# Absolute step sizes by DVE, one region of token slots per expert, three batches scattered early, and the zero fill on SyncE's queue

## The reference, cut to what matters

```
delta = jax.nn.softplus(dt_raw @ dt_w.T + dt_b)       # per batch, 512 channels x 512 steps
dA = jnp.exp(d_t[:, :, None] * A)
h = dA * h + d_t[:, :, None] * B_t[:, None, :] * x_t[:, :, None]
...
# top-1 mixture: each token goes to the expert with the largest gate logit
e = argmax(x @ gate_W + gate_b);  y = gelu(x @ W1[e] + b1[e]) @ W2[e] + b2[e]
```

## Time and profile before

| | us |
|---|---|
| three runs | 2758.61, 2760.15, 2762.63 |
| profiled execution, its own time | 2750.26 |
| its span | 2748.4 |
| PE busy in the span | 2504.7 (91%) |
| DVE busy | 1437.4 (52%) |
| ACT busy | 1101.9 (40%) |
| POOL busy | 709.6 (26%) |

### The profile page before, as it was taken

One profiled execution on the slowest core, in us unless ns is written; L12 is line 12 of the kernel. 1 busy time (PEld: TensorE's weight loads), 2 busy tenths in 40 slices (PEclk: granted clock), 3 DMA queues, 4 the chain that ended last, 5 costly groups with the idle time before them and its releaser, 6 DMA issues. The chain is left out here.

```text
span 2748.4 us, 40088 instructions
## 1 busy us (share of the span) xinstructions
PE 2504.7 (91%) x16440; PEld 1507.8 (55%) x16441; DVE 1437.4 (52%) x2067; ACT 1101.9 (40%) x1901; POOL 709.6 (26%) x388
## 2 busy tenths in 40 slices
PE   7759999999999999999949977999999998799998
PEld 4346533854375535753348854363453544588887
DVE  5557437952976357843811125555455654644442
ACT  3675335822664256533512223544445443011111
POOL 0148026910964056802720020000000000022222
PEclk9979999999999999999979987999999999899999
DMA  5541002100040003100059940010100102045553
GB/s 203 217 189 40 0 1 103 64 1 0 1 151 17 1 1 127 40 1 0 8 209 338 339 122 12 1 24 23 23 25 1 25 8 93 23 161 166 175 175 83
DMA packets 62127, 219.26 MB, mean 80 GB/s; under 512 B 12293, under 2 KB 28122, under 8 KB 45178
## 3 DMA queue, kind: packets, MB, share of 16 engines
q1 hardware_dynamic: 45802, 187.39, 18.9%
q0 software_dynamic: 9568, 18.75, 2.8%
q10 hardware_dynamic: 6576, 10.57, 1.1%
HBM read 172.50 MB, written 39.99 MB: 77 GB/s over the span
## 5 line engine op out<-in xcount | busy, mean ns | idle before, releaser
L653 PE MATMUL psum<-arena 128*128 128x512 f32 (+4 forms) x3776 | 1036.6, 427 | 59.9 <-ACT arena L1552 11.5
L653 PEld LDWEIGHTS psum<-arena 128*128 128x128 f32 x3776 | 617.4, 194 | 417.8 <-issue 312.5
L2539 POOL TENSOR_TENSOR arena<-arena 128x1024 f32<-128x1024 f32 x128 | 299.6, 2369 | 94.7 <-DVE arena L2019 79.9
L2019 DVE TENSOR_TENSOR_SCAN arena<-arena,psum 128x512 f32<-128x512 f32 x256 | 290.8, 1200 | 22.4 <-PE psum L809 14.6
L809 PEld LDWEIGHTS psum<-arena 128*128 128x128 f32 x2048 | 236.6, 193 | 49.3 <-ACT arena L1582 40.3
L809 PE MATMUL psum<-arena 128*128 128x128 f32 x2048 | 249.0, 279 | 2.0 <-issue 1.9
L2579 POOL DMA_INDIRECT arena<-xn,arena x32 | 31.6, 987 | 778.5 <-DVE arena L2481 771.5
L2546 POOL TENSOR_TENSOR arena<-arena 128x1024 f32<-128x1024 f32 x32 | 76.0, 2374 | 525.3 <-ACT arena L1681 525.3
L2127 DVE SCALAR_TENSOR_TENSOR arena<-psum,arena 128x1024 f32<-128x1024 f32 x128 | 155.9, 1244 | 93.9 <-PE psum L968 93.5
L1860 ACT ACTIVATE arena<-psum 128x256 f32<-128x256 f32 x128 | 49.1, 384 | 296.2 <-PE psum L653 296.2
L1681 ACT ACTIVATE arena<-arena 128x1024 f32<-128x1024 f32 x128 | 147.1, 1149 | 44.3 <-DVE arena L2127 43.0
(11 more groups left out here) (294 smaller groups left out, 3056.6 us busy)
## 6 DMA issues: line engine op xcount, KB each, us to landing
arena<-in_W SPq DMA_DIRECT2D x46, 1024.0 KB
arena<-c_rows SPq DMA_DIRECT2D x32, 512.0 KB, 4.1
arena<-in_Wg SPq DMA_DIRECT2D x16, 1024.0 KB, 4.9
arena<-in_Wu SPq DMA_DIRECT2D x16, 1024.0 KB, 7.5
arena<-in_Wd SPq DMA_DIRECT2D x16, 1024.0 KB, 9.9
arena<-in_xT SPq DMA_DIRECT2D x8, 512.0 KB, 6.0
zs_all<-arena SPq DMA_DIRECT2D x4, 1024.0 KB, 3.9
ut_all<-arena SPq DMA_DIRECT2D x4, 1024.0 KB, 8.8
```

What stands on the lines that cost most here:

```text
L653: r = mm(dst, w, x, start=i == 0, stop=i == len(pairs) - 1)
L2019: V.tensor_tensor_scan(hs[n % 3][:, c, :], dA[n % 2][:, c, :], bank[4 + c], 0.0, ALU.mult, ALU.add)\
L2539: nc.gpsimd.tensor_tensor(h, h, c_all[:, n % CBUFS, :].unsqueeze(1).broadcast_to([P, 2, L]), ALU.mult)\
```

## The change

**Step sizes.** ACT's four Abs of a round go; DVE does them as max(-v, v) directly behind L1962. In round 5, DVE instead of ACT copies batch 2's turned product, and DVE instead of POOL multiplies batch 3's delta by u, tile by tile behind each softplus.

**Slots.** `slots_x` becomes 135 tiles (17.7 MB instead of 3.1 MB): expert e has a region of its own of 2048 rows, so a token's row no longer depends on the counts of all tokens, only on those of earlier batches (`run`). Nine DMAs of 15 tiles each, issued by SP behind batch 0's loads of C, fill it with zeros. The store and load of `xn0` go; `xnn` has memory of its own. While batch b (1 to 3) is in its scans and attention, DVE picks experts and rows of batch b-1 (`pick_expert`, `place_tokens`), PE counts, and POOL scatters its four chunks. After the barrier only batch 3's 512 tokens are left: pick, count, place, four scatters.

**Expert loop.** A tile's rows start where the region says (`row_i`, read into a register), so the token tiles are now loaded by SP (`load_tokens`), ahead of the same tile's weights; ACT's queue has no part in it.

The diff, cut to its core:

```diff
+XT0, ZT0 = E0 * CH + E0 - 1, 9
-        slots_x = dram("slots_x", ((NT0 + 1) * P, D))
+        slots_x, slots_y = dram("slots_x", (XT0 * P, D)), dram("slots_y", (NT0 * P, D))
 # SP
+                if b == 0:
+                    sp.wait_ge(c_made.sem, 1)
+                    for z in range(ZT0):
+                        sp.dma_start(slots_x.rearrange("(z t p) d -> z p t d", z=ZT0, p=P)[z],
+                                     zero.unsqueeze(1).broadcast_to([P, XT0 // ZT0, D])).then_inc(stored_zero.sem, 16)
...
-            sp.dma_start(x_all, xn0.rearrange("c p d -> p c d")).then_inc(ld_x0.sem, 16)
-            sp.wait_ge(m_route.sem, 2)
+            sp.wait_ge(m_route.sem, 2 * B + 1)
+            def load_tokens(i, j):
+                r = row_tile(2 * i + j)
+                sp.wait_ge(g_full.sem, g_full.at(j - 1, i))
+                sp.dma_start(xg0[j], tiles_x[bass.ds(r, 1)].rearrange("a p d -> (a p) d")).then_inc(ld_g[j].sem, 16)
...
+            first = expert_of(0)
+            load_w1(first, 0)
+            sp.wait_ge(m_route.sem, 2 * B + 2)
+            sp.wait_ge(scattered.sem, 16 * CH)
+            sp.dma_start(xg0[0], tiles_x[bass.ds(row_tile(0), 1)].rearrange("a p d -> (a p) d")).then_inc(ld_g[0].sem, 16)
+            load_rest_of(first, 0)
+            load_tokens(0, 1)
+            load_expert(0, 1)
+            with sp.Fori(1, NT0 // 2) as i:
                 for j in range(2):
+                    load_tokens(i, j)
                     load_expert(i, j)
 # PE, behind keys_tile(3) of batches 1 to 3
+            def expert_counts(b):
+                pe.wait_ge(m_route.sem, 2 * b + 1)
+                ohf = oh16.rearrange("p c e -> p (c e)")
+                mm(bank[6][:, 0:NC * E0], low16, ohf, start=True, stop=True)
+                mm(bank[6][:, NC * E0:2 * NC * E0], ones16, ohf, start=True, stop=True).then_inc(m_counts.sem, 1)
 # ACT
-                if 0 <= b4:
+                if 0 <= b4 < B - 2:
...
-                        A_(a_ex[:, c, :], a_dl[:, c, :], ACT.Abs).then_inc(a_soft.sem, 1)
-                        wa(a_soft, 2 * c + 1, b3)
+                        wa(a_size, c + 1, b3)
                         A_(a_ex[:, c, :], a_ex[:, c, :], ACT.Exp, scale=-1.0).then_inc(a_soft.sem, 1)
...
-            act.dma_start(xg0[0], slots_x[0:P]).then_inc(ld_g.sem, 16)
-                    act.dma_start(xg0[1 - j], slots_x[(n + 1) * P:(n + 2) * P]).then_inc(ld_g.sem, 16)
 # DVE, behind L1962 and behind L1993
+                    for c in range(KI):
+                        wa(a_delta, c + 3, b3)
+                        V.scalar_tensor_tensor(a_ex[:, c, :], a_dl[:, c, :], -1.0, a_dl[:, c, :], ALU.mult, ALU.max)\
+                            .then_inc(a_size.sem, 1)
+                if s == B + 1:
+                    wa(a_st_duT, 0, B - 2)
+                    for c in range(KI):
+                        wa(a_duT_full, c + 1, B - 2)
+                        V.tensor_copy(a_duT[0][:, :, c * P:(c + 1) * P], bank[6 + c % 2].rearrange("p (q x) -> p q x", q=NC))\
+                            .then_inc(a_kept.sem, 1)
...
+                        if b3 == B - 1:
+                            if c == 0:
+                                wa(a_duT_full, 0, b3)
+                            wa(a_delta, c + 3 + KI, b3)
+                            V.tensor_tensor(a_du[:, c, :], a_dl[:, c, :], a_ut[b3 % 2][:, c, :], ALU.mult).then_inc(a_dur.sem, 1)
 # POOL
-            for b in range(B):
+            for b in range(B - 1):
...
+                if b == 1:
+                    pool.wait_ge(stored_zero.sem, 16 * ZT0)
+                if b >= 1:
+                    scatter(b - 1)
...
-            for c in range(CH):
-                pool.indirect_dma_start(slots_x, on(ap=slot_i[:, c:c + 1], axis=0), x_all[:, c, :], None)\
-                    .then_inc(scattered.sem, 16)
+            scatter(B - 1)
```

More of the change, by code:

```diff
@@ L217, in decoder_program @@
         zero, ones1 = take(D), take(P)
+        slot_i, slot_y = [take(CH).bitcast(u32) for _ in range(2)]
         shared_top = top[0]
@@ L275, in decoder_program @@
         a_bT, a_var, a_sd, a_r0, a_r1 = take(NC, NS), take(NC), take(NC), take(NC), take(NC)
+        xnn = take(NC, D)
+        oh, oh16, best, desc_w = take(CH, E0), take16(NC, E0), take(NC), take(NC, E0)
+        run, pre, slot_f = take(NC + 1, E0), take(NC, E0), take(CH)
         assert top[0] <= WORDS
@@ L760, in _ @@
             turn_du(B - 1)
[L761 removed]
+            wa(a_kept, 0, B)
             for b in range(B):
@@ L884, in transpose_p @@
                 def transpose_p(i):
+                    if i == 0 and b >= 1:
+                        pe.wait_ge(m_route.sem, 2 * b)
                     for g in range(2):
@@ L1037, in _ @@
             round_end(pe, rd_a, 0)
[L1040 to L1043, removed]
+            expert_counts(B - 1)
             def transpose_slots(j):
@@ new lines, in place_tokens @@
+            def place_tokens(b):
+                ranks, counts = [bank[6][:, i * NC * E0:(i + 1) * NC * E0].rearrange("p (c e) -> p c e", c=NC) for i in range(2)]
+                dve.wait_ge(m_counts.sem, b + 1)
+                for c in range(NC):
+                    link(m_step, V.tensor_tensor(run[:, c + 1, :], run[:, c, :], counts[:, c, :], ALU.add))
+                link(m_step, V.tensor_tensor(pre, run[:, 0:NC, :], ranks, ALU.add))
+                link(m_step, V.tensor_tensor(pre, pre, oh[:, b * NC:(b + 1) * NC, :], ALU.mult))
+                link(m_step, V.reduce_sum(slot_f[:, b * NC:(b + 1) * NC], pre, AX.X))
+                V.tensor_copy(slot_i[:, b * NC:(b + 1) * NC], slot_f[:, b * NC:(b + 1) * NC]).then_inc(m_route.sem, 1)
+                link(m_step, V.tensor_copy(run[:, 0, :], run[:, NC, :]))
@@ L2178, in _ @@
[L2178 to L2184 removed]
+            s3, tile = [P, NT0, E0], const[:, C_TILE:C_TILE + NT0]
@@ new lines, in _ @@
+            link(m_step, V.tensor_tensor(row_cmp, row_cmp, over(shift, s3, 1), ALU.mult))
+            link(m_step, V.reduce_max(row_f, row_cmp, AX.X))
+            V.tensor_tensor(row_i, row_f, tile, ALU.add).then_inc(m_route.sem, 1)
+            link(m_step, V.tensor_tensor(moved, oh, over(shift, [P, CH, E0], 1), ALU.mult))
+            link(m_step, V.reduce_sum(back, moved, AX.X))
+            V.scalar_tensor_tensor(slot_y, back, -float(P), slot_f, ALU.mult, ALU.add).then_inc(m_route.sem, 1)
@@ L2522, in _, with scatter @@
             pool.sem_inc(y0_free.sem, 2)
-            pool.wait_ge(c_made.sem, 1)
-            pool.dma_start(slots_x.rearrange("(t p) d -> p t d", p=P), zero.unsqueeze(1).broadcast_to([P, NT0 + 1, D]))\
-                .then_inc(stored_zero.sem, 16)
-            for b in range(B):
+            def scatter(b):
+                pool.wait_ge(m_route.sem, 2 * b + 2)
+                for c in range(NC):
+                    pool.indirect_dma_start(slots_x, on(ap=slot_i[:, b * NC + c:b * NC + c + 1], axis=0), xnn[:, c, :], None)\
+                        .then_inc(scattered.sem, 16)
+            for b in range(B - 1):
                 for c in range(KI):
```

144 lines of the change are left out of this document (73 added, 71 removed).

## The result

The changed kernel takes 2739.49 us (median of 6 runs, 2736.36 to 2741.85) against 2760.93 for the kernel before (6 runs): ratio 0.9921, 95% interval 0.9911 to 0.9932, or -21.4 us. The forecast was -25.5 (2734.7, range 2727 to 2749).

The account below looks back on a forecast made before the run. PE was taken as busy nearly everywhere, so only its idle places or added PE work count; -9.6 + 0.6 - 17.5 + 1.0 = -25.5 us gives 2734.7, own range 2728 to 2742, stated range 2727 to 2749.

Parts of the forecast that it names:

- Rounds 2 and 3, "sum 0": Prologue: four Abs leave ACT (-2.45) and join DVE ahead of the norm (+2.45); sum 0, at worst +2.5 per round.
- -9.6: Whole prologue, round 4 included: gain of 9.6 us, taken between 9.2 and 10.85.
- Round 4, -2.45: Prologue round without a norm chain: DVE's absolute values ready before ACT is free, so four Abs go, -2.45 us.
- Round 5: Prologue: softplus starts 9.2 us earlier, pairs of softplus and product take some 1.33 each, first scan 10.85 earlier.
- What is late next, the rows of C: Prologue's end: POOL's first product waits for C's rows, 14.8 us behind the store of delta, which moves by 9.2 only.
- Zero fill, 0: 17.7 MB of zeros on SP's queue take 107 us at 166 GB/s, within an empty 137 us stretch: cost 0.
- Rival 4: The zero fill holds batch 1's loads if under 129 GB/s; at 100 GB/s the time is 2775; chance 0.02.
- Early routing: Batches 0 to 2: DVE's picks and places hidden, PE's two small count products per batch cost +0.6 us in all.
- Start of the loop, -17.5: Expert loop's start: PE's first product at about 1401.5 instead of 1418.97, W2 last to arrive; ends -12 and -20.
- Loop, +1.0: Expert loop: W1 issued some 1.5 us later per tile, mostly hidden by the queue; +1.0, bounds -2 to +8.
- rival 3: Expert loop: every tile starts 1.5 us later from W1's delay, +33 instead of +1.0, time 2766.7; chance 0.06.
- The Trainium skill's rule on queue rows: Expert loop: engines go round between queue rows, so tokens on the weights' row would lose; the 6.4 us row shows little privilege.

Follow-up runs that it names:

- The variant with late values: Changed kernel with DVE's absolute values of rounds 2 and 3 behind the norm's small steps instead of ahead: 2731.98 us, ratio 0.9897.
- W1 behind the tokens: Changed kernel with tile 0's W1 issued behind its tokens, so no weights fly while the last scatters land: 2742.59 us, one run, no ratio.
- the test: Changed kernel with two more register reads ahead of W1 in each tile, so W1 is issued later: 2745.99 us, ratio 0.9942.
- the combination: Changed kernel with absolute values of rounds 2 and 3 behind the norm, and tile 0's b1, W2, b2 ahead of the scatters' wait: 2732.29 us, ratio 0.9888.

## Why the prediction was right, point by point

- **Rounds 2 and 3, "sum 0": right in its chain, wrong in its sum.** Round 2 was 0, as worked out. In round 3 the root came 2.2 later and the four Abs gave 2.6 back to ACT (2.45 worked out for both). Put at nothing was PE: it waits 2.75 for the norm, its clock falls, and batch 0's turn, whose copies stand ahead of Exp on ACT, ends another 1.5 later by that. The products behind softplus, at 115 to 120, then take 9.87 instead of 8.99, at a granted clock of 0.61 there instead of 0.91: 0.9 more. Together round 4 began 1.94 later. This is the whole difference between -9.6 and the -7.7 measured in the scans. The variant with late values shows the step's other side: 5.5 could be gained there.
- **Round 4, -2.45: right.** Softplus went from 1.94 late to 0.61 early: -2.55.
- **Round 5: right in its length, late by the 1.94.** Softplus 5.74 behind the complete v (5.7 worked out), a pair of softplus and product 1.33 (1.33).
- **What is late next, the rows of C: right.** The transfers take 14.65 behind the store of delta.
- **Zero fill, 0: right.** The size was too careful: 54 us instead of 107; the row of the old fill had been taken beside other traffic. Rival 4 is out.
- **Early routing: right in its places.** No wait of PE on the routing stands in its list in batches 1 to 3, and the two count products take 0.18 and 0.19 in the start's timeline. The +0.6 is too small to be seen.
- **Start of the loop, -17.5: mis-sized, it was -15.9.** Pick, count and place took 3.4, where 3.55 was worked out. The term that was short is the landing of the scatters: 1.5 behind the end before, 3.7 now beside W1, as W1 behind the tokens shows. Part of that was covered, since the forecast took the late end of its bounds; the last scatter came 0.5 later than worked out, and from W2's issue to PE's product it was 5.45 instead of 4.9. That W2 would be last was right.
- **Loop, +1.0: too small.** By the lengths of the loops it is +1 to +6, within the bounds of -2 to +8. Of rival 3's mechanism a part at most is real (6 to 9 of 24 in the test, 4.5 of them one tile). Not counted at all was the clock: in the combination, the tile whose wait was 2.86 lost another 3 to it.

The Trainium skill's rule on queue rows ("DMA: Bandwidth & Descriptors", "Queues, rings and completion order"), as the prediction cites it, would have the tokens lose something on the weights' row. The traces show no such loss. The issues of the changed kernel (KB, median us to landing):

```profile
arena<-slots_x SPq DMA_DIRECT2D x23, 128.0 KB, 4.3
```

On ACT's row it was 6.4, and 5.8 and 5.4 in the two variants with the tokens there again. Nor does PE wait for tokens in the changed kernel's loop: its only wait on them is the start's.

The steps in the traces sum to -7.7 + 0.6 - 15.9 + 3 = -20, the medians say -21.4. The forecast was right for its reasons in the large terms, 4 us too hopeful, from three small terms (round 3, the start, the loop) that all erred to the same side.

## What to carry to other kernels

An instruction moved to a less busy engine must be placed behind what other engines wait for there: the same four instructions on DVE cost 1.9 ahead of the norm's steps and gain 3.5 behind them. A wait that TensorE gets by such a move can cost more than its length: behind the 2.75 here the clock fell, and the next products took 1.5 longer. When a long serial tail is cut, the transfers that lay hidden under it become the next wait, and they then share the DMA engines with what is left of the tail. And before a term is read off the difference of two profiled spans, a second profile of the unchanged kernel shows how much of it is chance.

## What the runs showed of the hardware that was not expected

- ACT stood idle 3.9 to 6.0 us between a table load and the root behind it, at the same instruction in 13 of 14 profiled executions, and only in this first norm of layer 1, not in the later ones. No run was made on its cause; it stays open.
- Writes of zeros from one small tile ran at 340 to 368 GB/s in nine DMAs of 2 MB behind each other, where one of 3 MB had taken 18.5 us (166 GB/s) beside other traffic.
- Four scatters are in place 1.5 us behind the last one's end in a quiet DMA, 3.7 beside 1 MB of weights, 5.5 beside 2 MB.
- In five expert loops a single wait of PE of 2.03 to 4.21 us was followed by work at the lower clock level (a product of 3.73 us took 5.24 to 6.76), and so was the 2.75 in round 3; the loops' other waits for weights, up to 1.79, were not (3.84).
- 128 KB of tokens landed in a median of 3.9 to 4.6 us on the weights' own queue row, issued ahead of them, in nine executions, and in 5.4 to 6.4 on ACT's row in five.
